# Pass 1 with the projection in one block, and merge with pass 2 in one block, on one core

## What is computed

```python
x = x + 0.5 * _L0_ffn_ref(_layernorm(x), ...)      # pass 1
x = x + _L0_attn_ref(_layernorm(x), W_attn, b_attn, W_proj, b_proj, score_gain)
x = x + 0.5 * _L0_ffn_ref(_layernorm(x), ...)      # pass 2, same weights
# ffn: 8 experts of width 64, the best 2 chosen by sigmoid scores within 2 of 4 groups,
#      every expert computed and weighted by 0 or its weight, plus a shared expert of width 128
# attention: 16 heads of 8; s centred by its row mean, divided by its mean absolute value,
#      times score_gain; r = max(s, 0) ** 4 under a causal mask; att = r / sum(r); y = att @ v
```

## Time and profile before

| what | us |
|---|---|
| median of 3 runs (lowest, highest) | 471.69 (471.44, 473.25) |
| the profiled execution: time, span | 472.97, 471.2 |
| busy: PE, DVE, ACT, POOL | 411.9, 393.2, 323.6, 276.2 |
| TensorE's mean granted clock | 0.982 of full speed |

### The profile page before, as it was taken

How to read it: one execution, slowest core, us unless ns; L and a number is a source line. 1 busy time by engine, 2 the same in 40 slices (tenths; PEclk the granted TensorE clock), 3 DMA queues, 4 the chain that set the end, 5 groups by cost and what they waited for, 6 DMA issues and landing times. The chain is left out here.

```text
span 471.2 us, 13694 instructions
## 1 busy us (share of the span) xinstructions
PE 411.9 (87%) x5064; PEld 195.6 (42%) x5072; DVE 393.2 (83%) x928; ACT 323.6 (69%) x584; POOL 276.2 (59%) x204
## 2 busy tenths in 40 slices
PE   0779999783799999899999998999999886889996
PEld 0323444351244444444444444444444474224442
DVE  5886554887999999999999999999999987775443
ACT  3333222574999999999999999999999505322221
POOL 5960000023989999999999999999999700000000
PEclk9989999997999999999999999999999998899999
DMA  4300000015754206114033051051002100000001
GB/s 115 92 1 0 1 0 0 1 33 102 235 103 73 55 3 102 26 30 81 19 67 60 3 99 28 1 103 25 1 20 73 36 13 0 1 0 24 0 22 45
DMA packets 18237, 19.94 MB, mean 42 GB/s; under 512 B 4904, under 2 KB 10632, under 8 KB 18184
## 3 DMA queue, kind: packets, MB, share of 16 engines
q1 hardware_dynamic: 17832, 19.11, 18.9%
q10 hardware_dynamic: 352, 0.07, 0.1%
HBM read 13.02 MB, written 6.03 MB: 40 GB/s over the span
## 5 line engine op out<-in xcount | busy, mean ns | idle before, releaser
L1254 POOL TENSOR_TENSOR arena<-arena 128x1024 f32<-128x1024 f32 (+1 forms) x144 | 240.7, 1704 | 17.3 <-ACT arena L1226 16.6
L1187 DVE SCALAR_TENSOR_TENSOR arena<-bank,masks 128x512 f32<-128x512 f32 x288 | 179.9, 681 | 5.2 <-PE bank L1088 5.2
L1226 ACT ACTIVATE arena<-arena 128x1024 f32<-128x1024 f32 (+1 forms) x160 | 147.9, 958 | 1.0 <-DVE arena L1187 0.2
L1088 PE MATMUL bank<-Q,K 128*32 128x512 bf16 (+3 forms) x1536 | 96.7, 330 | 20.6 <-PEq L827 7.6
L1216 ACT ACTIVATE bank<-bank 128x1024 f32<-128x1024 f32 (+5 forms) x144 | 90.0, 625 | 4.8 <-PE bank L1088 4.2
L1088 PE MATMUL bank<-K,Q 128*32 128x512 bf16 (+3 forms) x1536 | 93.1, 329 | 0.0
L1193 DVE TENSOR_SCALAR_CACHE_REDUCE bank<-bank 128x896 f32<-128x896 f32 (+4 forms) x112 | 84.0, 779 | 0.0
L1125 PE MATMUL bank<-arena,Vq 128*32 128x512 f32 (+3 forms) x768 | 77.0, 486 | 0.0
L625 ACT ACTIVATE arena<-bank 128x512 f32<-128x512 f32 x40 | 23.9, 597 | 76.2 <-PE bank L500 76.1
L1088 PEld LDWEIGHTS bank<-Q,K 128*32 128x32 bf16 x1536 | 37.5, 96 | 87.0 <-issue 30.4
L726 DVE TENSOR_TENSOR arena<-arena,bank 128x512 f32<-128x512 f32 x40 | 27.4, 685 | 41.7 <-PE bank L504 41.5
(11 more groups left out here) (123 smaller groups left out, 344.3 us busy)
## 6 DMA issues: line engine op xcount, KB each, us to landing
Q<-q_parts SPq DMA_DIRECT2D x21, 192.0 KB
K<-k_parts SPq DMA_DIRECT2D x14, 128.0 KB
att<-arena SPq DMA_DIRECT2D x28, 64.0 KB, 1.6
K<-k_parts SPq DMA_DIRECT2D x7, 192.0 KB
K<-k_parts SPq DMA_DIRECT2D x18, 64.0 KB
X<-in_L_attn_x SPq DMA_DIRECT2D x4, 256.0 KB, 4.3
out_x<-X SPq DMA_DIRECT2D x4, 256.0 KB, 2.3
q_parts<-arena SPq DMA_DIRECT2D x3, 256.0 KB
```

The costliest lines, as they stand in the source:

```text
L1088: last = nc.tensor.matmul(m.bank[j:j + 32, at + lo:at + hi], left[par][:, g, blk * P + j:blk * P + j + 32], right[par][:, g, s0:s0 + hi - ...
L1187: nc.vector.scalar_tensor_tensor(Y(r, g)[:, y0:y0 + SPAN], m.bank[:, at:at + SPAN], 0.0, mask, ALU.max, ALU.mult).then_inc(relu_done, 1)
L1226: nc.scalar.activation(z, Y(r, g)[:, tile_low(r) - off(r):T - off(r)], ACT.Square)\
L1254: nc.gpsimd.tensor_tensor(z, z, z, ALU.mult).then_inc(fourth_p, 1)
```

## The change

Stages 1 to 3 become one block, `first_pass`; the merge and pass 2 (`Finish`) follow the attention's quads within its block, with no barrier between. In both, batch 0 goes ahead of batch 1, and each engine's list is written by hand, unrolled. The 20 down products of a pass are numbered n = 0 to 19, the shared chunk first in each span (`ORDER`); gate and up products (`item`) run ahead of them by `LEAD` = 5, and six hidden tiles are held instead of three. What each function does is as before; further:
- each span is normalised when its x has landed; the shared and expert weights are loaded first;
- gating takes eight tiles (a batch) at a time instead of four and twelve;
- the projection's q, k and v products are items of pass 1's queue; one half of v goes through ACT and GpSimd; all of batch 0's parts are stored together, batch 1's at the start of the attention's block (before: heads 0 to 3, and then the rest);
- `attention_constants` start after the gating of batch 1;
- in the merge, the first batch's sums are turned before the last rounds' sums are added; GpSimd adds the projection's bias to X in place of TensorE's products with the identity; batch 1 is inverted after batch 0 is normalised; in pass 2 ACT normalises span 2 and GpSimd span 3.

The core of the diff, pass 1 (TensorE, ACT, GpSimd, DVE in turn):

```diff
-        ffn(nc, m, sem, "f1", attention_constants, lambda sp: load_weights(m, sp, *weights), qkv_norm)
-        store_rest = project_qkv(nc, m, sem, qkv_norm, q_dram, k_dram)
...
+        first_pass(nc, m, sem, First(nc, m, sem, start, f1_norm, project), lambda sp: load_weights(m, sp, *weights))
+        attention(nc, m, sem, q_dram, k_dram, att_dram, project, out)
...
+    LEAD, HELD = 5, 6
+    ORDER = [NCH, 0, 1, 2, 3]
+    LAST = NSPAN * HCH
...
+        self.items = ffn(0, 17) + [("qk", 0), ("qk", 1)] + ffn(17, 20) + [("v", 0), ("qk", 2), ("qk", 3), ("v", 1)]
...
+    def new_items(self, n):
+
+        if n == 0 or n == 5 or n == 10:
+            return range(0)
+        if n < 15:
+            r = self.LEAD + n - 1 - n // HCH
+            return range(r, r + 1)
+        r = 17 if n == 15 else n + 3
+        return range(r, r + 2 if n == 15 else r + 1)
...
+        pe.wait_ge(self.start.made, self.start.READY)
+        transpose(0)
+        transpose(1)
+        pe.wait_ge(m.gate_loaded, 16 * 2)
+        logits(0)
+        item(0)
+        turn_scores(0)
+        item(1)
+        transpose(2)
+        item(2)
+        pe.wait_ge(s.xnT_ready, 3)
+        transpose(3)
+        item(3)
+        turn_weights(0)
+        item(4)
+        for n in range(self.LAST):
+            if self.routed(n):
+                spread_weights(n)
+            for r in self.new_items(n):
+                item(r)
+            if n == 0:
+                logits(1)
+            if n == 1:
+                turn_scores(1)
+            if n == 5:
+                turn_weights(1)
+            if n == 14:
+                pe.wait_ge(self.wT_ready, NSPAN)
+                project.transpose(pe, 0, self.attention_xt_ps[0])
+                pe.wait_ge(self.x_added, 2)
+                project.transpose(pe, 1, self.attention_xt_ps[1])
+            if n == 19:
+                pe.wait_ge(project.norm.xnT_ready, 2)
+                project.transpose(pe, 2, self.attention_xt_ps[2])
+            if n and not self.routed(n):
+                turn_back(self.span_of(n) - 1)
+            down(n)
+        turn_back(NSPAN - 1)
+        item(23)
+        pe.wait_ge(project.norm.xnT_ready, 3)
+        project.transpose(pe, 3, self.attention_xt_ps[3])
+        item(24)
+        item(25)
...
+        self.start.scalar(act)
+        for i in range(2):
+            root(s, i)
+            norm_last_tile(nc, m, s, act, i)
+        take(0)
+        take(1)
+        root(s, 2)
+        root(s, 3)
+        nc.scalar.activation(m.table[:, 1:2], m.eps[:, :], ACT.Sigmoid)
+        sigmoid(0)
+        norm_last_tile(nc, m, s, act, 2)
+        norm_last_tile(nc, m, s, act, 3)
+        item(0)
+        item(1)
+        take(2)
+        item(2)
+        take(3)
+        item(3)
+        act.wait_ge(self.wT_zeroed, 1)
+        take_weights(0)
+        item(4)
+        for n in range(self.LAST):
+            if n and not self.routed(n):
+                take_out(self.span_of(n) - 1)
+            for r in self.new_items(n):
+                item(r)
+            if n == 0:
+                nc.scalar.activation(m.table[:, 2:3], m.eps[:, :], ACT.Sigmoid)
+                sigmoid(1)
+            if n == 5:
+                take_weights(1)
+            if n == 11:
+                nc.scalar.activation(m.table[:, 3:4], m.eps[:, :], ACT.Sqrt)
+                root(project.norm, 0)
+                root(project.norm, 1)
+            if n in (12, 13):
+                norm_last_tile(nc, m, project.norm, act, n - 12)
+            if n == 14:
+                project.take(act, 0, self.attention_xt_ps[0])
+                project.take(act, 1, self.attention_xt_ps[1])
+            if n == 15:
+                act.wait_ge(self.silu_ready, 19)
+                project.high_part(act, "q", 0)
+            if n == 16:
+                act.wait_ge(project.k_centred, 1)
+                project.high_part(act, "k", 0)
+            if n == 17:
+                nc.scalar.activation(m.table[:, 4:5], m.eps[:, :], ACT.Sqrt)
+                root(project.norm, 2)
+                project.middle_part(act, "q", 0)
+            if n == 18:
+                norm_last_tile(nc, m, project.norm, act, 2)
+                project.middle_part(act, "k", 0)
+        project.take(act, 2, self.attention_xt_ps[2])
+        take_out(NSPAN - 1)
+        nc.scalar.activation(m.table[:, 5:6], m.eps[:, :], ACT.Sqrt)
+        item(23)
+        root(project.norm, 3)
+        norm_last_tile(nc, m, project.norm, act, 3)
+        project.take(act, 3, self.attention_xt_ps[3])
+        item(24)
+        act.wait_ge(self.silu_ready, 25)
+        project.high_part(act, "q", 1)
+        act.wait_ge(project.k_centred, 2)
+        project.high_part(act, "k", 1)
+        item(25)
+        project.middle_part(act, "q", 1)
+        project.middle_part(act, "k", 1)
...
+        pool.wait_ge(self.parts_ready, 2)
+        attention_constants(nc, self.m, sem, pool)
+        minus = nc.gpsimd.tensor_tensor
+        project.rest_part(pool, minus, "q", 0)
+        project.low_part(pool, minus, "q", 0)
+        project.low_part(pool, minus, "k", 0)
+        pool.wait_ge(self.silu_ready, 23)
+        project.v_full(minus, 0, project.v_raw).then_inc(project.v_out, 1)
+        project.rest_part(pool, minus, "q", 1)
+        project.low_part(pool, minus, "q", 1)
+        pool.wait_ge(self.silu_ready, 26)
+        project.v_full(minus, 2, project.v_raw).then_inc(project.v_out, 1)
+
...
+        self.start.moments(dve, 0, s)
+        norm_vector(nc, m, s, dve, 0)
+        self.start.moments(dve, 1, s)
+        norm_vector(nc, m, s, dve, 1)
+        self.start.moments(dve, 2, s)
+        self.start.moments(dve, 3, s)
+        dve.wait_ge(m.gate_loaded, 16 * 2)
+        norm_vector(nc, m, s, dve, 2)
+        norm_vector(nc, m, s, dve, 3)
+        scores(0)
+        pick_groups(now)
+        item(0)
+        better_experts(now, range(1, E))
+        pick_experts(now)
+        item(1)
+        weigh(now)
+        item(2)
+        item(3)
+        item(4)
+        for n in range(self.LAST):
+            if self.routed(n):
+                scale(n)
+            for r in self.new_items(n):
+                item(r)
+            if n % HCH == 1 and n > 1:
+                add_to_x(self.span_of(n) - 1)
+                moments(self.span_of(n) - 1)
+            if n == 1:
+                scores(1)
+                pick_groups(later)
+            if n == 2:
+                better_experts(later, range(1, E // 2))
+            if n == 3:
+                better_experts(later, range(E // 2, E))
+                pick_experts(later)
+            if n == 4:
+                weigh(later)
+            if n == 9:
+                project.signs(dve, link)
+            if n in (12, 13):
+                norm_vector(nc, m, project.norm, dve, n - 12)
+            if n == 15:
+                dve.wait_ge(self.prod_ready, 19)
+                project.centre_k(link, 0)
+            if n == 17:
+                norm_vector(nc, m, project.norm, dve, 2)
+                project.rest_part(dve, nc.vector.tensor_tensor, "k", 0)
+        add_to_x(NSPAN - 1)
+        moments(NSPAN - 1)
+        item(23)
+        norm_vector(nc, m, project.norm, dve, 3)
+        item(24)
+        dve.wait_ge(self.prod_ready, 25)
+        project.centre_k(link, 1)
+        item(25)
+        project.rest_part(dve, nc.vector.tensor_tensor, "k", 1)
+        project.low_part(dve, nc.vector.tensor_tensor, "k", 1)
```

The core of the diff, end of the attention's block (TensorE, ACT from n = 0 on, GpSimd, DVE):

```diff
+            finish.slope(dve)
             quads(dve, body)
-            merge.vector(dve)
+            finish.vector(dve)
...
+            pe.wait_ge(upper_a, (NQUAD - 1) * NA + count(by_a, (NR - 1, 0)))
+            finish.turn_upper(pe, 0)
             pe.wait_ge(relu_done, NQUAD * NRELU)
             pe.wait_ge(upper_v, NQUAD * NV)
             pe.wait_ge(upper_a, NQUAD * NA)
-            merge.turn_upper(pe, 0)
-            for what, r in (("relu", 3), ("power", 3), ("relu", 4)):
+            finish.turn_upper(pe, 1)
+            for what, r in (("relu", 3), ("power", 3), ("relu", 4), ("power", 4)):
                 for piece in pieces(NQUAD - 1, what, r):
                     add_piece(*piece)
-            merge.turn_upper(pe, 1)
-            for piece in pieces(NQUAD - 1, "power", 4):
-                add_piece(*piece)
-            merge.tensor(pe, sums, sums_out, NQUAD)
+            finish.spread_inverse(pe, 0)
+            finish.spread_inverse(pe, 1)
+            finish.project(pe, 0)
+            finish.project(pe, 1)
+            finish.pick_last_quad(pe, sums, sums_out)
+            finish.tensor(pe)
...
+        transpose(0)
+        transpose(1)
+        logits(0)
+        item(0)
+        turn_scores(0)
+        item(1)
+        self.spread_inverse(pe, 2)
+        self.spread_inverse(pe, 3)
+        item(2)
+        item(3)
+        turn_weights(0)
+        item(4)
...
+                item(r)
+            if n == 0:
+                self.project(pe, 2)
```

(76 more changed lines are left out.)

1291 lines of the change are left out of this document (732 added, 559 removed).

## The result

| kernel | median us (lowest to highest) | runs | mean clock of the profiled run |
|---|---|---|---|
| before | 472.99 (471.44 to 474.17) | 5 | 0.982 |
| changed | 467.90 (466.43 to 468.83) | 5 | 0.978 |

The ratio is 0.989, 95% interval 0.986 to 0.993. The change makes the kernel faster by 1.1% where 4% was forecast; 467.9 lies outside the range of 444 to 461. Run again later it came to 469.19 against 472.53, ratio 0.993 (0.990 to 0.995). The profiled execution of the changed kernel is its fastest, 466.43 with a span of 464.5.

What follows compares the result with a forecast made beforehand. It took attention as full on DVE and ACT, FFN passes as TensorE-bound, the rest as seams. From 471.2 us of span, 10.5 and 8.4 came off: 452.3, plus 0.5 gave 453 us, range 444 to 461.

Steps and rivals of the forecast that it cites:

- the allowance of 0.5: Added to the 452.3 us span for the median, since before's median lay 0.5 us above its profiled span.
- Step 1: Start to first down product of pass 1: from 31.2 to 26.5 us, 4.7 us won.
- Step 2: First to last down product of pass 1: from 56.6 to 59.8 us, 55.3 TensorE work plus 4.5 lost.
- Step 6: First to last down product of pass 2: 50.4 us of work plus 2.5 lost, ending at 458.0 against 466.4.
- The two terms for lost time: TensorE's lost time inside the passes: 4.5 us in pass 1 and 2.5 us in pass 2.
- TensorE idle for more than 6 us inside a pass: A sign, stated in advance, that the prediction's account was wrong.
- The collision of the six tile scalings with GpSimd's constants: Pass 1, n = 12 and 13: DVE scalings at 0.87 instead of 0.27, 3.6 us, of which 2 taken.
- Step 3: Last down product of pass 1 to attention: from 26.0 to 17 us; attention starts at 103.3, 10.5 us won.
- the lock: DVE and GpSimd excluding each other on shared ports; for centring k beside GpSimd's subtraction, 0 to 2 us, 0.6 taken.
- Steps 4 and 5: Attention's end to scores, 28.7 to 22.1 us, 1.8 added for half clock; scores to first down product, 9.75 to 11.7.
- in-order queues bite: Rival, chance 0.17: DVE's extra work and ACT's table loads expose themselves in the passes, 453 + 9 = 462 us.
- Code that does not arrive in time: Rival, chance 0.04: unrolled spans wait for instruction fetch; 0.5 us per step is 20 us, at 0.6 about 476.

Runs made afterwards that it cites:

- a0_again: The changed kernel once more, unaltered, for a second trace: 469.19 us, ratio 0.993 to before.
- e2_apart: The changed kernel with batch 1's four subtractions and span 3's values done by DVE alone, none by GpSimd: 464.20 us, ratio 0.983 to before.
- e1_order: The changed kernel with DVE's extra work put ahead of the item's product, and pass 1's batch 1 gating a step later: 459.12 us, ratio 0.971 to before.
- e8_lead4: e1_order with pass 1's ACT tables and DVE tile scalings moved, and pass 2's lead cut from five items to four: 456.71 us, against 457.34 with five.
- e9_best: e1_order and e2_apart edits, moved tables and scalings, earlier score turning, unread TensorE products at start, tail, merge and before attention: 449.13 us, ratio 0.951 to before.

## Why the prediction was wrong

The direction was right, and so was the way in which the seams shrink. What failed is the account of how DVE's work is hidden inside a pass, and a price for the two engines' collision in the tail. 12.2 us of span are missing, and 2.7 more in the median, which lies 3.4 above the profiled span where the forecast put 0.7. Of these 2.7, about 1.5 come from the profiled execution of the changed kernel being the fastest of five, and about 1.3 from that of before being slower than its median, which had made the allowance of 0.5 too small. The start of the fastest one was early by the clock's chance. The mean clock of the four others is 0.972 to 0.973 against its 0.978; which falls of the clock they had, no trace shows.

- **Step 1**, first down product: right to 0.1 us in the first trace. That was a lucky one: scores at 15.70 there, 16.55 in a0_again and 17.19 in e2_apart, where TensorE's first up product ran at half its speed (1.92 us for two instructions that take 1.02). The step had no term for the clock, although the first down product of before, 1.57 us, was in the earlier trace rows.
- **Step 2** holds the failed sentence: that the gating, the additions to X and the statistics on DVE, 3.1 to 3.4 us in a step of 2.79, are mostly covered by "the five items of lead", with 0.5 us for what is not. **Step 6** takes it over: its 2.5 us hold nothing for the gating and the additions from n = 6 on. The lead covers the products. It does not cover the scales: a scale's spread stands right behind the down product of the step before, and the scale itself stands in order behind whatever DVE's list has ahead. The slack there can be read from the timeline: it has 1.2 us behind the product, and 1.9 us of work stood in front of it. e1_order moved the work by one place and won 4.2 and 3.6 us, e8_lead4 then took lead away and lost nothing. With the order mended pass 1 took 59.37 against the 59.8 forecast, pass 2 53.85 against 52.9. The two terms for lost time were some 4 us too small each; by the table they make 8.35 of the 12.2, of which e1_order won back 7.8. In that pass 2 TensorE's waits for other engines sum to only 1.9 us, below the 2.5 allowed. So the 0.95 that it still took above the forecast is not lost time of this kind; no run takes it apart. The third down product of pass 2 in before, 1.31 us late behind the same mixture, was in the prediction, but under a rival. The prediction's own sign of a wrong account, TensorE idle for more than 6 us inside a pass, is just met in pass 1 (63.55 - 57.50 = 6.05).
- The collision of the six tile scalings with GpSimd's constants, 2 us in step 2, did not happen: three took 0.85 at 65.33, GpSimd's constants having ended at 62.4. That error was on the other side.
- **Step 3**, 17 us, took 20.7: 1.4 by the clock (3.44 against 1.96 for L476), the rest by the lock. I gave the lock 0.6 for one instruction; it held up three on the two engines, and e2_apart won 2.96 us by doing without GpSimd. Without it the tail was 16.35, below the forecast. That the loads of batch 0 would be hidden was right: attention was released by its block. They were later than the 94 of the prediction, though: SP issued the last of them at 97.8, and the DMA queues were idle from 102 on, 9 us ahead of attention.
- **Steps 4 and 5**: right within 0.4 us, with the half clock expected there; holding it gives 1.9.
- **Rivals**: "in-order queues bite" (462, 0.17) named DVE's extra work, and the time was 6 us beyond even that. But its 9 us were priced as table loads alone, and those are not what was lost: e1_order left all of them in place and won 7.8 us. They show only where something of DVE's waits behind them in order, as the 0.79 us at n = 17. Code that does not arrive in time played no part: the changed kernel's two waits put down to a remote queue (1.58 us at 27.89, 0.40 at 444.46) stand where the trace lacks the record of the spread waited for, no down product waited behind them, and a0_again, which has all those records, shows no such wait. The gap at the loop's entry that spoke for this rival in the trace of before is one of 0.91 us, put down to ACT's taking of the weights (L614) in both passes. In the range the queues' term and the lock should have stood together, since nothing keeps them from happening both: 453 + 8.4 + 2.4 (3.0 less the 0.6 already in) would have been 464.

## What to carry to other kernels

A lead of n items protects only what is truly made n ahead. For each instruction on an in-order engine ask what limits how early it can run: the place of its input's producer in another engine's list, as here, or a buffer. Where that leaves less than a step, its slack is what counts, and extra work belongs behind it and ahead of the instruction that does have lead. Issuing the spread earlier, or with a second bank, is the other way out; no run here tries it. And do not split a chain of elementwise steps in SBUF between DVE and GpSimd where it is on the critical path: here one engine alone was 3 us faster than both.

## What was not expected

- Two short idle times of TensorE, 1.28 us each, cost another 1.6 us each in one trace of the same kernel and nothing in the other, through the granted clock. The spread of the runs, highest less lowest, fell from 1.9 us to 0.5 in e1_order, where of these two waits 0 and 0.4 us are left, and to 0.16 in e9_best, where other idle times are filled too.
- At the start the clock's column says 1.00 while the products take what they take at 0.50: up product 1.92 us for two instructions at 14.62 in e2_apart, 1.02 at 14.25 in the changed kernel. There the lengths have to be read, not the column. The trace's list of the granted clock has no entry ahead of the first rise, 13.93 us in the changed kernel and 17.08 in e2_apart, and the column reads 1.00 where there is none. Among the traces without added products at the start a late rise goes with a late first down product: 13.9 with 26.4 to 26.5, 15.7 with 27.3, 17.1 with 27.9.
- A sum of two numbers per partition took 1.7 us longer beside a GpSimd subtraction, and the centring of k (1024 numbers per partition) 1.8 us longer: what the lock costs goes by the length of the other engine's instruction, 2.12 us here, and not by that of the one held up.
